# Last attention of a two-layer decoder: scores from split halves of queries and keys

## The reference, cut to what matters

```python
def _L1_xattn_ref(query, key, value, Wq, bq, Wk, bk, Wv, bv, Wo, bo):
    H, dk = 16, 32
    def proj(x, W, b):
        y = jnp.einsum('bsd,ed->bse', x, W) + b
        return y.reshape(B, -1, H, dk).transpose(0, 2, 1, 3)
    Q, K, V = proj(query, Wq, bq), proj(key, Wk, bk), proj(value, Wv, bv)
    scores = jnp.einsum('bhqd,bhkd->bhqk', Q, K) / np.sqrt(dk).astype(jnp.float32)
    attn = jax.nn.softmax(scores, axis=-1)
    out = jnp.einsum('bhqk,bhkd->bhqd', attn, V)
    return jnp.einsum('bsd,ed->bse', out.transpose(0, 2, 1, 3).reshape(B, -1, D), Wo) + bo
```

## Time and profile before

| | us |
|---|---|
| three runs, median | 3399.25 |
| the profiled execution's own time | 3404.09 |
| its span, first to last instruction | 3402.3 |
| TensorE busy (share of span) | 3081.5 (91%) |
| VectorE busy | 2084.2 (61%) |
| ScalarE busy | 1396.6 (41%) |
| GpSimd busy | 1316.7 (39%) |

### The profile page before, as it was taken

How to read it: one execution, slowest core, us unless ns; L and a number is a source line. 1 busy time by engine, 2 the same in 40 slices (tenths; PEclk the granted TensorE clock), 3 DMA queues, 4 the chain that set the end, 5 groups by cost and what they waited for, 6 DMA issues and landing times. The chain is left out here.

```text
span 3402.3 us, 72145 instructions
## 1 busy us (share of the span) xinstructions
PE 3081.5 (91%) x23816; PEld 2301.2 (68%) x23832; DVE 2084.2 (61%) x5258; ACT 1396.6 (41%) x4594; POOL 1316.7 (39%) x1982
## 2 busy tenths in 40 slices
PE   7999999999997999999969877877779996999997
PEld 6788888888885777887744333333357774777775
DVE  7676676666664888888852111122156666888885
ACT  5344444444443555555541111110021114777774
POOL 3454554454452344444410000000022223888886
PEclk9999999999998999999989899898889998999998
DMA  3000000000102111121359999999731113222221
GB/s 121 32 18 31 24 18 25 31 18 18 37 13 77 61 50 49 55 68 49 118 230 424 427 426 425 426 425 426 322 114 57 57 49 113 76 82 76 88 83 35
DMA packets 145368, 448.74 MB, mean 132 GB/s; under 512 B 11604, under 2 KB 62808, under 8 KB 124824
## 3 DMA queue, kind: packets, MB, share of 16 engines
q1 hardware_dynamic: 126808, 429.56, 32.6%
q10 hardware_dynamic: 18496, 18.35, 1.5%
HBM read 395.45 MB, written 52.43 MB: 132 GB/s over the span
## 5 line engine op out<-in xcount | busy, mean ns | idle before, releaser
L505 POOL TENSOR_TENSOR cross_prob<-cross_prob,cross_rsum 128x128 f32<-128x128 f32 (+1 forms) x512 | 255.2, 528 | 347.9 <-DVE cross_rsum L952 347.6
L505 POOL TENSOR_TENSOR self_prob<-self_prob,self_rsum 128x128 f32<-128x128 f32 (+1 forms) x512 | 287.1, 586 | 243.4 <-DVE self_rsum L952 243.3
L1944 POOL TENSOR_TENSOR last_prob<-last_prob,last_rsum 128x256 f32<-128x256 f32 x512 | 298.6, 614 | 92.5 <-DVE last_rsum L2280 90.2
L758 ACT ACTIVATE self_prob<-self_S,self_neg_max 128x128 f32<-128x128 f32 (+1 forms) x512 | 211.6, 424 | 207.5 <-DVE self_neg_max L944 207.4
L1600 POOL MEMSET norm_minus_half<- 128x2 f32 x1 | 0.1, 100 | 738.7 <-POOLq L53 738.7
L499 POOL TENSOR_TENSOR self_QK_T<-self_QK_T,self_turned 128x512 f32<-128x512 f32 x128 | 166.3, 1300 | 280.5 <-DVE self_QK_T L868 278.8
L2159 ACT ACTIVATE last_prob<-last_S,last_neg_max 128x256 f32<-128x256 f32 x512 | 237.8, 490 | 20.6 <-DVE last_neg_max L2276 20.6
L758 ACT ACTIVATE cross_prob<-cross_S,cross_neg_max 128x128 f32<-128x128 f32 (+1 forms) x512 | 209.7, 427 | 76.3 <-DVE cross_neg_max L944 75.3
L1489 DVE COPY experts_hidT<-experts_T 128x512 f32<-128x512 f32 x32 | 22.1, 691 | 283.5 <-PE experts_T L1380 283.5
L2276 DVE TENSOR_REDUCE last_neg_max<-last_S 128x2 f32<-128x512 f32 x256 | 165.9, 681 | 32.3 <-PE last_S L2070 32.1
L2090 PE MATMUL last_T<-last_ident,last_prob 128*128 128x128 f32 x1024 | 161.8, 281 | 19.1 <-DVE last_probT L2285 15.3
(11 more groups left out here) (324 smaller groups left out, 9702.4 us busy)
## 6 DMA issues: line engine op xcount, KB each, us to landing
moe_w<-in_L_ffn_w SPq DMA_DIRECT2D x32, 4096.0 KB, 34.7
late_x<-in_L_ffn_w SPq DMA_DIRECT2D x32, 4096.0 KB, 39.6
front_spare<-in_ctx SPq DMA_DIRECT2D x32, 512.0 KB, 11.2
front_x_t<-in_x SPq DMA_DIRECT2D x16, 512.0 KB, 3.6
self_res<-in_x SPq DMA_DIRECT2D x16, 512.0 KB, 3.6
x<-self_res SPq DMA_DIRECT2D x16, 512.0 KB, 2.8
front_x_t<-x SPq DMA_DIRECT2D x16, 512.0 KB, 4.8
cross_res<-x SPq DMA_DIRECT2D x16, 512.0 KB, 3.7
```

What stands on the lines that cost most here:

```text
L505: ins = pool.tensor_tensor(pr, pr, rsum[:, h, t:t + 1].to_broadcast([P, KQ[t]]), ALU.mult)
L758: ins = act.activation(prob[:, h % NP, SOFF[t]:SOFF[t] + KQ[t]], SC[h % G][:, SOFF[t]:SOFF[t] + KQ[t]], ACT.Exp, bias=neg_max[:, h, t:t + ...
L1944: ins = pool.tensor_tensor(pr, pr, rsum[:, h, t:t + 1].to_broadcast([P, S]), ALU.mult)
```

## The change

1. `QT` (float32) becomes two float32r tensors `QTs`, high and low; `KT` stays as it is loaded, and two more, `KTs`, are added.
2. `scores` issues for each head and row tile three float32r matmuls in a row (high*high, high*low, low*high), in place of one in float32. It waits for `k_lo` (the low half of the keys) in place of the load.
3. ScalarE's query step writes the high half and no longer frees the bank; a new VectorE step `Q` writes the low half from the bank and frees it.
4. A new step `K(g)+` on both: ScalarE copies the next batch's keys into the high half, VectorE subtracts it from the keys into the low half. Both operands of this subtraction and its result are in SBUF.
5. SyncE waits for `k_lo` in place of `s_full` before it loads the next keys of a group.
6. The scale 1/sqrt(32) moves from the query step into the split of `wq`, done once.

```diff
         "ACT": (
-                "take13- exp2 z2- exp3 take15- z3- Q2 exp4 exp5 exp6 Q3 take1 exp7 X0+ X1+ take3 exp8 exp9 exp10 exp11 Q0+ "
-                "take5 exp12 Q1+ take7 exp13 z0 exp14 take9 exp15 F0- F1- take11 exp0+ z1 exp1+"),
+                "take13- exp2 z2- exp3 take15- z3- Q2 exp4 K0+ exp5 exp6 Q3 take1 exp7 K1+ X0+ X1+ take3 exp8 exp9 exp10 exp11 K2+ Q0+ "
+                "take5 exp12 Q1+ take7 exp13 z0 exp14 take9 exp15 F0- F1- take11 exp0+ z1 K3+ exp1+"),
         "DVE": (
-                "max3 take14- inv1 inv2 z2- stats+ max4 max5 take0 z3- max6 max7 apply+ inv3 inv4 O0- take2 X0+ inv5 max8 max9 "
-                "inv6 X1+ max10 inv7 max11 inv8 inv9 O1- take4 fstats- inv10 max12 take6 max13 max14 inv11 max15 take8 z0 fapply- "
-                "inv12 inv13 inv14 take10 max0+ max1+ max2+ take12 z1 inv15 inv0+ G0- G1-"),
+                "max3 take14- inv1 inv2 z2- stats+ max4 max5 take0 z3- Q2 max6 max7 K0+ Q3 apply+ inv3 inv4 O0- take2 X0+ inv5 max8 max9 K1+ "
+                "inv6 X1+ max10 inv7 max11 inv8 inv9 O1- take4 fstats- inv10 max12 take6 Q0+ max13 max14 Q1+ K2+ inv11 max15 take8 z0 fapply- "
+                "inv12 inv13 inv14 take10 max0+ max1+ max2+ take12 z1 K3+ inv15 inv0+ G0- G1-"),
...
-        QT = ph.sb("QT", [P, NG, S])
+        QTs = [ph.sb(f"QT{i}", [P, NG, S], F32R) for i in "hl"]
+        KTs = [ph.sb(f"KT{i}", [P, NG, S], F32R) for i in "hl"]
...
-                        sp.wait_ge(s_full, n * H + G * key[1] + G)
+                        sp.wait_ge(k_lo, n * NG + key[1] + 1)
                         load_keys(following, key[1])
...
-                pe.wait_ge(keys_in[g], n * 16 + 16)
+                pe.wait_ge(k_lo, n * NG + g + 1)
...
-                        mm = pe.matmul(SC[i][:, t * S:(t + 1) * S], QT[r:r + d_head, g, t * P:(t + 1) * P], KT[r:r + d_head, g, :],
-                                       start=True, stop=True, tile_position=(r, 0))
+                        for j, (q, k) in enumerate(((0, 0), (0, 1), (1, 0))):
+                            mm = pe.matmul(SC[i][:, t * S:(t + 1) * S], QTs[q][r:r + d_head, g, t * P:(t + 1) * P], KTs[k][r:r + d_head, g, :],
+                                           start=(j == 0), stop=(j == 2), tile_position=(r, 0))
...
-                release(act.activation(QT[:, g, :], A[BANK[key]][:, 0:S], ACT.Identity, bias=bq_c[:, g:g + 1], scale=SCALE), key, n)
+                act.activation(QTs[0][:, g, :], A[BANK[key]][:, 0:S], ACT.Identity, bias=bq_c[:, g:g + 1]).then_inc(q_hi, 1)
+
+            def keys_hi(n, g):
+                act.wait_ge(keys_in[g], n * 16 + 16)
+                after(act, s_full, n, H, G * (g + 1 - NG))
+                act.activation(KTs[0][:, g, :], KT[:, g, :], ACT.Copy).then_inc(k_hi, 1)
...
+            def queries_lo(key, n):
+                g = key[1]
+                dve.wait_ge(q_hi, n * NG + g + 1)
+                release(dve.scalar_tensor_tensor(QTs[1][:, g, :], A[BANK[key]][:, 0:S], bq_c[:, g:g + 1], QTs[0][:, g, :],
+                                                 ALU.add, ALU.subtract), key, n)
+
+            def keys_lo(n, g):
+                dve.wait_ge(k_hi, n * NG + g + 1)
+                dve.tensor_tensor(KTs[1][:, g, :], KT[:, g, :], KTs[0][:, g, :], ALU.subtract).then_inc(k_lo, 1)
```

More of the change, by code:

```diff
@@ L1854, in last_phase @@
         a_free = [ph.sem(f"a_free{i}") for i in range(2)]
-        (ident_in, b_in, r_in, w8_in, w_hi, w_lo, x_ok, res_in, res_b, stored, ln, ln_pow, a_full, x_hi, scaled, s_full,
+        (ident_in, b_in, r_in, w8_in, w_hi, w_lo, x_ok, res_in, res_b, stored, ln, ln_pow, a_full, x_hi, scaled, q_hi, k_hi, k_lo, s_full,
          max_ok, exp_ok, rsum_ok, norm_ok, t_full, pt_dve, pt_act, pv_ok, pool_const, with_eps, with_eps_l, z_hi, z_ok, fl, fl_pow, biased,
@@ L1858, in last_phase @@
             ph.sem(n) for n in (
-                "ident_in b_in r_in w8_in w_hi w_lo x_ok res_in res_b stored ln ln_pow a_full x_hi scaled s_full "
+                "ident_in b_in r_in w8_in w_hi w_lo x_ok res_in res_b stored ln ln_pow a_full x_hi scaled q_hi k_hi k_lo s_full "
                 "max_ok exp_ok rsum_ok norm_ok t_full pt_dve pt_act pv_ok pool_const with_eps with_eps_l z_hi z_ok fl fl_pow biased "
@@ L2138, in high_weights @@
                 act.wait_ge(w_in[i], 16)
-                act.activation(high[:, :, :], w_stage[:, i, :, :], ACT.Copy).then_inc(w_hi, 1)
+                act.activation(high[:, :, :], w_stage[:, i, :, :], ACT.Copy, scale=(SCALE, 1.0)[i]).then_inc(w_hi, 1)
             def release(ins, key, n):
@@ L2191, in body @@
                         queries(key, n, off)
+                    elif key[0] == "K":
+                        keys_hi(n, key[1])
                     elif key[0] == "exp":
@@ L2210, in low_weights @@
                 dve.wait_ge(w_hi, i + 1)
-                dve.tensor_tensor(parts[1][:, :, :], w_stage[:, i, :, :], parts[0][:, :, :], ALU.subtract).then_inc(w_lo, 1)
+                dve.scalar_tensor_tensor(parts[1][:, :, :], w_stage[:, i, :, :], (SCALE, 1.0)[i], parts[0][:, :, :], ALU.mult, ALU.subtract).then_inc(w_lo, 1)
             def norm_stats(n):
@@ L2303, in body @@
                         output(key, n)
+                    elif key[0] == "Q":
+                        queries_lo(key, n)
+                    elif key[0] == "K":
+                        keys_lo(n, key[1])
                     elif key[0] == "max":
```

## The result

In five runs of each kernel on one chip the changed kernel takes 3415.18 us (3412.64 to 3419.2), the kernel before 3399.27 (3394.81 to 3401.97). The ratio is 1.0048, with a 95% interval of 1.0033 to 1.0062: slower by 16 us, and over the 0.2% (6.8 us) under which the prediction calls a change none. The forecast was 3402. The time lies inside the range of 3388 to 3420, and "slower" had a chance of 0.38 against 0.45 for "same".

A forecast was written before the change was run, and what follows sets the result against it. TensorE sets the pace (31.06 of 32 us busy); its 0.6 us gain a batch is lost to VectorE waits at T5 and T9. 1.5 for 15 batches plus 1.5 at the start, about +3 on 3399.25, gives 3402 us; range 3388 to 3420.

The forecast's parts named there:

- the scores: TensorE's score groups: 24 records in six rounds, 1.01 us for 1.15, giving back 0.6 us a batch.
- the case of 3480: Rival at TensorE's scores: products of one head hold up the others, 2.4 us a group, 3480 us; chance 0.05.
- `Q2 K0+ Q3` add 0.40 + 0.35 + 0.40 = 1.15 between `z3-` and `O0-`: VectorE's new work there fits its 1.24 us of idle time, so is hidden; only 0.05 us for the bank.
- the new keys' subtraction: VectorE's low half of keys, both operands in SBUF: can wait up to 0.39 us behind a GpSimd instruction.
- At T5 +0.06: `K1+` on VectorE delays `take4`, so TensorE's T5 loses S2's gain and 0.06 us more.
- At T9 +0.35: `Q0+ Q1+ K2+` ahead of `take8` on VectorE make TensorE's T9 0.35 us later after S3's end.
- its +0.1: Net loss taken per batch since waits of `K1+`, `K2+` and semaphores are uncertain: 1.5 us in 15 batches.
- The forecast by itself: Main case, VectorE's waits eating TensorE's gain: 3402 us, own range 3394 to 3409, chance 0.44.
- the rival of the long wait: `K3+` on VectorE falls behind a long GpSimd instruction, TensorE stands about 0.95 us a batch: 3416 us; chance 0.24.
- VectorE has room: VectorE's new low halves, 3.0 us a batch, fit in the sum into its 5.07 us of idle time.
- ScalarE's and SyncE's parts: ScalarE's key copies, 1.5 us of 7.47 idle, are free; SyncE's loads zero; bound 0.1 us a batch each.
- The start: `K0+ K1+` ahead of the first `X0+`, and first scores waiting for a low half: +1.5 us.

The follow-up runs named there:

- experiment 2: Changed kernel without VectorE's low halves; high halves stand in for them in the same three products, ScalarE frees the bank: 3393.21 us, ratio 0.9978.
- Experiment 1: Changed kernel with `apply+` moved ahead of `K0+` and `Q3` in VectorE's list: 3406.01 us, ratio 1.0019.
- Experiment 5: Changed kernel with GpSimd's output bias addition on two columns only, the rest of that sum left out: 3407.37 us, ratio 1.0021.
- experiment 10: Changed kernel, VectorE: `apply+` before `Q3`, `K0+` before `take2`, `K1+` behind `inv10`, `K2+` behind `take10`; ScalarE: `K0+`, `Q3` earlier: 3397.96 us, ratio 0.9994.
- experiment 6: Changed kernel with VectorE's `K2+` moved from ahead of `take8` to behind `take10`: 3411.36 us, ratio 1.0038.
- experiment 3: Changed kernel with all halves made, but scores as one float32 product a head, of the high halves: 3429.89 us, ratio 1.0092.
- experiment 8: Changed kernel, VectorE: `K0+` before `take0`, `K1+` before `take2`, `K2+` behind `take10`, `apply+` before `Q3`; ScalarE: `K0+`, `Q3` earlier: 3402.95 us, ratio 1.0009.

## Why the prediction was right or wrong

**Right: the scores.** The four groups are 0.58 us a batch shorter for 0.6 forecast, and 0.43 of it is left in the batch when VectorE has no new work (experiment 2). Four heads run abreast with three products of one head in a row; the case of 3480 did not come. The Trainium skill's rule ("TensorE: Matmul & The Clock Gate", Part 3, The mechanism) that matmuls start strictly in program order is not what these rows show: the 1st, 4th, 7th and 10th product in the program start together, and 24 matmuls of 0.27 us and more are done in 1.00.

**Wrong, and the step that failed: "`Q2 K0+ Q3` add 0.40 + 0.35 + 0.40 = 1.15 between `z3-` and `O0-`; VectorE idles 1.24 there. Hidden."** The idle time was `O0-`'s, and `O0-`'s sum on VectorE does hide it. But `apply+` stands between `Q3` and that idle time, and TensorE waits for `apply+` at `X0+`; the air ahead of `X0+`, 0.93 us, was never worked out. Besides, 1.15 took no wait of `Q3` for ScalarE, 0.66 us. The price is 0.96 us at `X0+`, of which 0.16 comes back at T2, so 0.8 a batch, 12 us. Experiment 1 shows the cause: with `apply+` first 0.73 of it goes.

**A term that was missing: `F0-`.** 0.35 us a batch, 5 us, because the shift brought L2267 to within 0.01 us of the start of a GpSimd operation. The prediction looked for such waits only at the new keys' subtraction; an old instruction with its operands in SBUF met one. Experiment 5 takes it away, and the batch falls from 33.05 to 32.74; a wait of the same kind, some 0.2 us a batch, is what is left in experiment 10.

**Two terms too large.** At T5 +0.06 with S2's gain gone was forecast (0.21 in all); +0.02 was measured, and the gain stayed. Experiment 1, with `X0+` mended, keeps it too, so it is not a gift of the late `X0+`; why `K1+` costs so little there stays open. At T9 +0.35 was forecast, +0.21 measured; experiment 6 shows that it was `K2+`. The steps of the forecast end at 0.0 a batch, and its +0.1 was an allowance on top. With these terms they give +0.8 + 0.35 - 0.19 - 0.14 = 0.82, against 0.85 measured; T14 is 0.80 late and the next `Q2` 0.85.

**That the time lies in the range is luck.** The forecast by itself reached to 3409; the range went on to 3420 for the rival of the long wait (3416), and what slowed the kernel was neither. **That rival came near the time by another way.** `K3+` never exceeded 472 ns in the changed kernel. Its mechanism is real, as experiment 3 shows (1.52 us, 0.8 a batch), and it decides on less than 0.15 us: 0.04 behind GpSimd's start `K3+` waits, 0.10 ahead of it it doesn't. "VectorE has room" held in the sum: experiment 10 has the same work on VectorE, is no slower than the kernel before, and loses 0.18 us a batch against experiment 2, which has none of it. **Right as well:** ScalarE's and SyncE's parts cost little by themselves in their places. Experiment 2 has them, and it keeps 0.43 of 0.58, so they cost 0.15 a batch at most. The start was not tested apart.

## What to carry to other kernels

An idle time covers only what is queued directly ahead of the instruction that waited; for each instruction between the added work and that wait, ask who waits for its result. When a split needs work on two engines, the second half waits for the first, so price it by when the first engine comes to it. Count room by the place too: against experiment 2 the same instructions cost 1.28 us a batch or 0.18, by where they stood. And once the places are moved, look again at every operation between SBUF tiles, the old ones too: a shift of 0.1 us decides whether it meets one of GpSimd.

## What the runs showed of the hardware

- A VectorE operation between SBUF tiles took longer when a GpSimd one had just begun, or began with it: 0.42 became 1.52 us with 1.24 of the GpSimd instruction left (experiment 3), 0.54 became 0.90 with 0.61 left (`F0-`'s L2267), and 0.42 became 0.83 with 0.54 left (`K1+` in experiment 8). The delay is what was left of the GpSimd instruction less 0.13 for the keys' subtraction and less 0.25 for L2267. The Trainium skill ("SBUF — State Buffer", section "SBUF: two separate sides") has a shared port pair held for a whole instruction; these rows agree but for that margin, for the subtractions with two SBUF inputs. L2267 and L2234 have one input tile and met it as well; which of the page's cases they are, no run here shows. `K1+` in experiment 8 waited for the third of four L1945 only, not for the fourth that followed at once; that one took 0.80 in place of 0.61, so the delay goes both ways. So it does when VectorE is a little ahead: in the same experiment `K0+` began 0.03 ahead of an L1945 and kept its 0.41, while that L1945 took 0.86; `apply+`, as much ahead of another, was the one that waited.
- Float32r products of 256 columns on quarters of the array came in rounds 0.12 us apart, as on the whole array, so three of them took 0.93 us a group where a float32 product took 1.08.
